# A graph layer, a mixer and an FFN in one kernel: a new order of TensorE's products and of loads, with one FFN block moved from the tail into the main steps

## What is computed

```python
xn = layernorm(x)
agg = segment_sum(edge_weight * xn[src], dst)              # gathered rows, summed per node
g   = relu(((1 + eps) * xn + agg) @ W1.T + b1) @ W2.T + b2
h   = relu(batchnorm(conv(log_map(xn), w_qkv)))            # mixer: one position, so the convolutions are products
t   = log_map(exp_map(h));  s = pointwise(depthwise(t));  q, k, v = split(concat(t, s))
o   = (v k^T) q / (sum(v) + 1e-15)
x2  = x + g + exp_map(o @ w_res + b_res)
x3  = layernorm(x2)
w   = x3 @ wr + br;  chosen = the top half of the nodes by w, less one
out = x2 + x3 + where(chosen, w * (gelu(x3 @ w1 + b1) @ w2 + b2), 0)
```

## Time and profile before

| | |
|---|---|
| median of 3 runs | 2584.17 us (2583.99 to 2586.97) |
| the profiled execution's own time | 2587.11 us |
| its span, first to last instruction | 2584.8 us |
| mean granted TensorE clock | 0.981 of full speed |
| PE busy | 2406.0 us, 93% |
| DVE busy | 1740.2 us, 67% |
| POOL busy | 1662.4 us, 64% |
| ACT busy | 1431.4 us, 55% |
| main loop | from 187.4 to 2457.2 us |

### The profile page before, as it was taken

The page is one execution under the profiler, slowest core; times in us unless marked ns, Lnnn a source line. Parts: engine busy times, 40 slices in busy tenths (PEclk is TensorE's granted clock), DMA queues, the critical chain, the costliest instruction groups (busy, mean ns, idle before and its releaser), DMA issues.

```text
span 2584.8 us, 44369 instructions
## 1 busy us (share of the span) xinstructions
PE 2406.0 (93%) x13536; PEld 1795.6 (69%) x13536; DVE 1740.2 (67%) x5895; ACT 1431.4 (55%) x3219; POOL 1662.4 (64%) x1834
## 2 busy tenths in 40 slices
PE   4688999999999999999999999999899999999896
PEld 4665677776777776777776677777677777666686
DVE  7857576576665767657667676676766766767557
ACT  3545565565655656556555565565655656556431
POOL 1236777677776777777767777676776776777500
PEclk9889999999999999999999999999999999999998
DMA  6733444434444344443443444434444343344338
GB/s 208 252 103 103 131 116 116 117 114 131 115 118 116 113 117 123 122 121 114 116 117 114 131 115 116 118 112 125 115 122 119 114 124 110 114 132 116 88 118 283
DMA packets 225215, 327.42 MB, mean 127 GB/s; under 512 B 80845, under 2 KB 168510, under 8 KB 224956
## 3 DMA queue, kind: packets, MB, share of 16 engines
q0 software_dynamic: 84656, 231.94, 30.9%
q1 hardware_dynamic: 140300, 92.36, 12.1%
HBM read 285.70 MB, written 38.45 MB: 125 GB/s over the span
## 4 chain that ended last, share of the span: by engine, by line
PE 57%; DVE 37%; DMA 3%; issue 2%; ACT 1%; POOL 0%; SPq 0%; DVEq 0%
PE qkv L1451 14%; PE bank L1463 13%; PE bank L1356 11%; DVE rings L1155 6%; PE bank L1416 3%; PE bank L1425 3%; PE bank L1400 3%; DVE bank L1175 3%; DVE work L1180 3%; DVE work L1169 3%; DVE bank L1174 2%; PE qkv L1380 2%; DVE bank L1168 2%; DVE bank L1179 2%; DVE work L1178 2%
## 5 line engine op out<-in xcount | busy, mean ns | idle before, releaser
L958 POOL DMA_INDIRECT rings<-xn_dram,window x1715 | 1634.6, 953 | 694.3 <-issue 398.4
L1356 PE MATMUL bank<-rings 128*64 128x256 f32 x4410 | 662.7, 393 | 10.1 <-DMA rings<-xn_dram,window 7.1
L1155 DVE TENSOR_SCALAR rings<-iota,window_dst,window 128x64 f32<-128x64 f32 (+1 forms) x1715 | 490.1, 341 | 216.6 <-PE bank L1356 205.6
L1356 PEld LDWEIGHTS bank<-rings 128*64 128x64 f32 x4410 | 319.1, 137 | 276.2 <-issue 105.5
L1451 PE MATMUL qkv<-work,ffn_weights 128*128 128x256 f32 x1568 | 369.7, 384 | 0.0
L1463 PE MATMUL bank<-ffn_weights,work 128*128 128x256 f32 x1568 | 359.5, 382 | 0.0
L1463 PEld LDWEIGHTS bank<-ffn_weights,work 128*128 128x128 f32 x1568 | 293.8, 190 | 54.0 <-issue 16.2
L1048 ACT ACTIVATE work<-qkv,fb 128x256 f32<-128x256 f32 x392 | 160.1, 473 | 305.0 <-PE qkv L1451 304.5
L1451 PEld LDWEIGHTS qkv<-work,ffn_weights 128*128 128x128 f32 x1568 | 292.1, 191 | 52.5 <-ACT work L1048 16.2
L1370 PE MATMUL bank<-resident,weights 128*128 128x256 f32 x1176 | 285.6, 386 | 0.3
L1370 PEld LDWEIGHTS bank<-resident,weights 128*128 128x128 f32 x1176 | 217.7, 192 | 45.3 <-ACT work L1061 19.2
(11 more groups left out here) (261 smaller groups left out, 3267.2 us busy)
## 6 DMA issues: line engine op xcount, KB each, us to landing
rings<-xn_dram,window POOLq DMA_INDIRECT x1715
xn_dram<-work SPq DMA_DIRECT2D x14, 896.0 KB, 7.9
work<-xn_dram SPq DMA_DIRECT2D x49, 256.0 KB, 3.0
work<-in_x SPq DMA_DIRECT2D x48, 256.0 KB
out<-work SPq DMA_DIRECT2D x48, 256.0 KB
work<-in_x SPq DMA_DIRECT2D x7, 896.0 KB, 5.9
rings<-in_x SPq DMA_DIRECT2D x6, 896.0 KB, 10.0
rings<-out SPq DMA_DIRECT2D x6, 896.0 KB, 9.1
```

Of the source, the lines that this page charges most:

```text
L958: nc.gpsimd.indirect_dma_start(out=msg[G_ % RING][:, :], out_offset=None, in_=xn_dram[:, :], in_offset=bass.IndirectOffsetOnAxis(ap=window ...
L1155: v.tensor_scalar(one_hot(i, k, 0, len(quarters)), iota[:, quarters[0] * H:(quarters[-1] + 1) * H], window_dst[b][:, k:k + 1], window[b][: ...
L1356: te.matmul(agg[h][side * H:(side + 1) * H], one_hot(i, k, REACHES[k].index(q), 1), msg[gathered % RING], start=first, stop=n == STEP_PROD ...
```

## The change

FFN blocks run in all steps from 2 on but 11, 23, 35 and 47: 43 in the loop and 6 in the tail. TensorE's `W1`, `W2`, second `mix_qkv` and first `mix_outT` come three edge products earlier (at 2, 8, 15 and 19 instead of 5, 11, 18 and 22); everything behind stays where it was, under new names. `ffn_turn` goes ahead of `tail_supT`. ScalarE copies x3T behind the seed of half 0 instead of ahead of `mix_exp`. VectorE's `x` and `y` come earlier, `f`, the first `combine` and the second `c` later; with the first `combine` at position 9, the reciprocal at 8 now stands ahead of it. SP issues `load_x(i - 1)` ahead of `load_xn(i)`.

```diff
--- before.py
+++ after.py
@@ -806,7 +806,7 @@
 
         FFN_AT, m_next = {}, 0
         for i in range(2, NS):
-            if i % 9 != 8:
+            if i % 12 != 11:
                 FFN_AT[i], m_next = m_next, m_next + 1
         LATE = list(range(m_next, NS))
         ran = lambda i: sum(k <= i for k in FFN_AT)
@@ -814,9 +814,8 @@
         def x3_rows(m, h):
             return h0T[:, h, 2 * m * P:2 * (m + 1) * P]
 
-        PE_AT = dict(w1=5, w2=11, qkv=18, outT=22, ft=26, h1=30, late=34, hid=38, y=41)
-        DVE_AT = dict(scale=(6, 12), out=(8, 16), c=(15, 22), ft=(17, 36), sup=0, n4=1, f=5, y=6, x=4,
-                      combine=(7, 15), rstd=20, tail_out=(25, 30), stage=22)
+        PE_AT = dict(w1=2, w2=8, qkv=15, outT0=19, ft0=26, h2=30, outT1=34, ft1=38, hid3=41, y2=45)
+        DVE_AT = dict(scale=(6, 12), out=(8, 16), c=(15, 23), ft=(17, 36), sup=0, n4=1, f=7, y=4, x=3, combine=(9, 15), rstd=20, tail_out=(25, 30), stage=22)
 
         def after(eng, s, v):
 
@@ -869,8 +868,8 @@
             sp.wait_ge(bn_ready, 1)
             load_xn(sp, 0)
             for i in range(1, NS):
+                load_x(sp, i - 1)
                 load_xn(sp, i)
-                load_x(sp, i - 1)
                 if i + 1 < NS:
                     load_window(sp, i + 1)
                 store_rows(sp, i - 1)
@@ -1069,12 +1068,12 @@
                 if j >= 0:
                     mix_n4_seed(j, tail)
                     tail_supT(j)
-                    if m is not None:
-                        ffn_x3T(m)
                     mix_exp(j)
                 mix_norms(i, 0)
                 mix_s_seed(i, 0, mix)
                 if j >= 0:
+                    if m is not None:
+                        ffn_x3T(m)
                     tail_g1(j)
                 mix_v(i, 0, mix)
                 mix_norms(i, 1)
@@ -1475,10 +1474,10 @@
                         done += 1
 
                 mix_qkv(i, 0)
+                if m is not None:
+                    ffn_turn(m, i)
                 if j >= 0:
                     tail_supT(j)
-                if m is not None:
-                    ffn_turn(m, i)
                 edges_to(PE_AT["w1"])
                 if j >= 0:
                     tail_w1(j)
@@ -1489,30 +1488,32 @@
                 mix_qkv(i, 1)
                 if i < NS - 1:
                     mix_h1(i + 1, 0)
-                edges_to(PE_AT["outT"])
+                edges_to(PE_AT["outT0"])
                 mix_outT(i, j, 0)
-                edges_to(PE_AT["ft"])
+                edges_to(PE_AT["ft0"])
                 mix_ft(i, j, 0)
                 if i < NS - 1:
                     mix_h1(i + 1, 1)
-                edges_to(PE_AT["h1"])
+                edges_to(PE_AT["h2"])
                 if i < NS - 1:
                     mix_h1(i + 1, 2)
-                edges_to(PE_AT["late"])
+                edges_to(PE_AT["outT1"])
                 mix_outT(i, j, 1)
                 if m is not None:
                     ffn_hidden(m, 0, i)
                     ffn_hidden(m, 1, i)
-                edges_to(PE_AT["hid"])
+                edges_to(PE_AT["ft1"])
                 mix_ft(i, j, 1)
                 if m is not None:
                     ffn_hidden(m, 2, i)
-                edges_to(PE_AT["y"])
+                edges_to(PE_AT["hid3"])
                 if m is not None:
                     ffn_hidden(m, 3, i)
+                if m is not None:
                     ffn_project(m, 0, i)
+                if m is not None:
                     ffn_project(m, 1, i)
-                edges_to(STEP_PRODUCTS)
+                edges_to(PE_AT["y2"])
                 if m is not None:
                     ffn_project(m, 2, i)
                     ffn_project(m, 3, i)
```

## The result

The changed kernel takes 2571.09 us (median of 5 runs, 2568.62 to 2576.11), the kernel before 2584.17 (5 runs beside it, 2583.48 to 2586.97): ratio 0.995, 95% interval 0.9936 to 0.9965. That is 13 us faster; 2572 had been predicted. The profiled execution of the changed kernel took 2568.62 us, its span is 2566.5.

What follows compares the result with a forecast made beforehand. VectorE's chain was taken to set FFN steps and DMA the tail's end. +8.7 - 12.9 - 6.4 - 1.0 - 0.3 = -11.9 on 2587.11 gave 2575.2, less 2.94 for the median 2572 us; 8 in 10: 2560 to 2585.

Steps and rivals of the forecast that it cites:

- The block: Main loop: one more main step holds an FFN block, costing 8.69 us at the old order's prices.
- The tail's -0.3: Tail with one late block fewer: 0.3 us gained out of 0 to 2.7, as stores queue on full DMA engines.
- D: Rival, tail: late blocks, not DMA, set the end, so the block's 15 us go; 2557 us, chance 0.05.
- FFN steps: 38 plain main steps: new product order lets VectorE's chain start earlier, 0.34 us a step, 12.9 us in all.
- Pairs: Step without FFN and the next: earlier W1, x and turn save 1.6 us a pair, 6.4 us for four.
- Steps 0 to 2: Loop's first steps, same pattern as a step without FFN and its successor: 1 us gained, 0 to 2.
- A: Rival, FFN steps: VectorE's chain stays put since x3T delays ScalarE as W1's wait did; 2585.5 us, chance 0.15.
- B: Rival: chain stays put and GpSimd's gathers limit the shortened pair, so the block is unpaid; 2592.9 us, chance 0.08.
- C: Rival, FFN steps: TensorE's order counts, its 0.43 us slot and part of two waits go; 2558 us, chance 0.12.

Runs made afterwards that it cites:

- the cut reloads: Changed kernel with the six reloads of the tail's last pass cut from seven row tiles to one, engines' work and waits kept: ratio 0.9916 to the kernel before.
- the kernel with supT first: Changed kernel with the old steps for FFN blocks and supT's transposes back ahead of x3's turn: 2543.48 us, ratio 0.984 to the kernel before.

## Why the prediction was right

**The sum** was -11.9 us against the profiled execution; the medians differ by 13.1. That the two lie so close is partly luck, as the terms show.

**The block** (+8.7): the new steps alone cost +5.4 us (3.1 to 7.8) by the ratio and 7.9 in the loop of the profile. Right in sign and somewhat too high at the old order; at the new order the block costs some 8.5 us (0.995 against 0.9917). The tail's -0.3 measured -0.2 in the kernel after; the 2.04 us of wait for the last late block, which "can go" by the prediction, stayed. The rival in which the tail pays (D) falls by the tail of the new steps alone (0.6 us shorter, not 15) and by the cut reloads.

**FFN steps** (-0.34 each): -0.32, so -12.2 us for 38. The path was as foretold: W1 earlier, with it g1 (which had waited 0.63 us for W1) and V's copy, then the reciprocal. That starts at 9.65 (9.68 foretold); the waits moved to W1 (0.17, from 0.75 less the 0.58 of the kernel with supT first; 0.2 foretold), second qkv (0.27; 0.3) and turns (0.34 and 0.56; 0.4 each); ft waits no more. But the agreement to 0.02 us hides two errors that cancel in the mean. The short steps gained 0.50: 0.33 up to the first om (15.75 instead of 16.08), and 0.13 because the one-hots and the norm between it and the second combine take less time (2.40 us from start to start; before 2.53). The long steps gained 0.15, since gathers now hold up VectorE elsewhere. The prediction had priced GpSimd only by its total of gathers, not by the time at which each runs. The prediction also counted the one-hot out of the chain, with combine behind the reciprocal, as 0.22 us of the gain. Against the old order the sum holds, but combine left in front would have done better (46.94 us a step). Each of the other parts undone by itself (x3T's place, the load order, one more product ahead of W1) takes back no more than 0.06 us of the mean step, and the turn's place undone gains; TensorE's earlier W1, W2 and second qkv were not undone together, so that they carry the gain rests on the rows.

**Pairs** (-1.6 each): -1.77 at 84.40, with a wrong reason among two. "x turns up 3.09 us late from its DMA, which held up f and the scale behind it" is the step that failed: with the late x back, pairs are as short. What is left is the order: in the mean of the pairs the step without FFN takes 31.65 instead of 32.36, its second qkv starting at 10.49 instead of 11.13, and the step behind it 52.76 instead of 53.82, 0.7 of that in the wait for sup. That it all comes from TensorE's earlier W1 was not tried by itself. The prediction left out that the clock falls in a pair: the step behind has a granted clock of 0.97 or 0.94 in each of them, before and after, 1.00 in all plain steps. In it TensorE runs at 1.2 instead of 2.4 GHz for 3.4 or 6.8 us, from about the end of its wait for sup on. It may make part of the scatter between pairs (85.57 to 86.79 before, 83.85 to 84.72 after); the two ranges do not meet.

**Steps 0 to 2** (-1): 127.2 instead of 128.4 us, but 129.4 in the kernel with the cut reloads, whose loop is the same code; the gain is within that scatter.

**Rivals.** A: FFN steps are not at 47.4. B: pairs shrank, and products waited for gathers for 12.0 us in all (7.1 before); but three small instructions on GpSimd per step cost a pair 1.2 us, so it stood close. GpSimd by line in a pair, as the earlier trace rows:

```profile
L957 POOL DMA_INDIRECT rings<-xn_dram,window x65 | 62.7, 965 | 22.0 <-issue 15.2 <-PE bank L1355 6.7
```

C: a slot added cost nothing (the chain without a gap, which spoke against C, is 17.5 us by the earlier trace rows and not 17.4). D: see the block.

## What to carry to other kernels

Price the engine that stands beside the path by when its instructions run, not by its total: list the lengths of all repeats of a step, and if they fall in two kinds, compare one of each row by row before believing a mean. Put first whatever starts the longest chain through several engines, even where another instruction would fill the time as well: supT ahead of the turn came with 0.6 us less in each FFN step. A wait that ends last on one instruction is worth only what the next wait of the same engine leaves; 150 us of waits for x were worth nothing.

## What was not expected of the hardware

Some of VectorE's instructions take longer beside GpSimd's gathers. Over the main loop of the kernel after, a one-hot takes 0.31 us in general (0.34 with 128 columns), in the mean 0.45 when it starts 0.4 to 0.5 us behind the start of a gather, 0.42 at 0.5 to 0.6 and 0.35 at 0.6 to 0.7. The small norm (L1230) takes 0.17 us at 0.44 and 0.40 at 0.53 to 0.54. Both are TENSOR_SCALAR; the rows of other operations that look longer (L475 at 0.33, the reciprocal at 0.81) overlap a stretched row in front of them. The 256-wide combine that reads PSUM (L1222) stays at 0.41, but only 7 of its 96 starts lie at 0.4 to 0.6. A shift of 0.05 us between the two engines decides over 0.36 us of a step.

The ends tell more than the means. All 160 one-hots of 64 columns that start 0.44 to 0.64 us behind a gather of ordinary length (under 0.97 us) end 0.96 to 1.00 us behind its start, 155 of them at 0.96 to 0.97, and the small norms that start at 0.53 to 0.76 all end at 0.94. No one-hot of 64 columns that starts under 0.38 us behind a gather takes over 0.32. So VectorE is held up to a fixed moment late in the gather and not over the whole of it. The Trainium skill, "SBUF — State Buffer", SBUF: two separate sides, says that VectorE and GpSimd share one pair of ports, and that a VectorE instruction in a mode that uses both ports, or with two inputs in SBUF (this only against a GpSimd instruction that reads SBUF), and one of GpSimd shut each other out of it, the first to start holding the pair for the whole instruction. That one waits for the other agrees with the rows; that the pair is held over the whole of a gather's 0.95 us does not. What a gather does in that stretch stays open.
